# Relative attention: turning one PSUM bank's distances by transposes and the other's by products with the identity

## The reference, cut to what matters

```python
q, k, v = x @ Wq + bq, x @ Wk + bk, x @ Wv + bv        # then split into 8 heads
attn1 = jnp.einsum('bhqd,bhkd->bhqk', rq, rk)
attn2 = jnp.einsum('bhqd,qkd->bhqk', rq, rk2)          # rk2 = rel_k[clipped distance k - q]
attn = jax.nn.softmax((attn1 + attn2) * (1.0 / math.sqrt(c)), axis=-1)
w1 = jnp.einsum('bhqk,bhkd->bhqd', attn, rv)
w2 = jnp.einsum('bhqk,qkd->bhqd', attn, rv2)
out = (w1 + w2).transpose(0, 2, 1, 3).reshape(b, t, c) @ Wo + bo
```

## Time and profile before

| what | value |
|---|---|
| median of 3 timed runs | 2436.7 us (2436.6 to 2438.9) |
| profiled execution, its own time | 2430.69 us |
| its span | 2428.9 us |
| busy share of the span, PE / DVE / ACT / POOL | 90% / 74% / 70% / 24% |
| mean granted clock of TensorE | 0.922 |
| image loop, from its first matmul to DVE's last maximum | 1489.57 to 1615.57 us |

### The profile page before, as it was taken

The page is one execution under the profiler, slowest core; times in us unless marked ns, Lnnn a source line. Parts: engine busy times, 40 slices in busy tenths (PEclk is TensorE's granted clock), DMA queues, the critical chain, the costliest instruction groups (busy, mean ns, idle before and its releaser), DMA issues. The chain is left out here.

```text
span 2428.9 us, 55288 instructions
## 1 busy us (share of the span) xinstructions
PE 2174.1 (90%) x22198; PEld 1519.2 (63%) x22198; DVE 1793.3 (74%) x2576; ACT 1708.1 (70%) x3089; POOL 586.3 (24%) x262
## 2 busy tenths in 40 slices
PE   6689999999999999998746979988599999999998
PEld 3554444444444444443235859865499999999998
DVE  4348999899998998988656344544688888888887
ACT  3478888888888888888742245751677777777776
POOL 0234545454544544444200011430000000000000
PEclk9589999999999999999857977999599999999999
DMA  6287777787787777787510000000321221222220
GB/s 177 74 236 215 217 202 225 214 229 199 219 228 219 214 213 218 218 225 206 121 56 1 2 9 2 2 23 19 121 70 62 73 74 66 73 74 74 74 74 20
DMA packets 113320, 305.66 MB, mean 126 GB/s; under 512 B 20479, under 2 KB 57465, under 8 KB 112554
## 3 DMA queue, kind: packets, MB, share of 16 engines
q1 hardware_dynamic: 113066, 302.13, 43.1%
HBM read 169.11 MB, written 80.65 MB: 103 GB/s over the span
## 5 line engine op out<-in xcount | busy, mean ns | idle before, releaser
L750 ACT ACTIVATE la_hid<-ps,la_b 128x904 f32<-128x904 f32 (+1 forms) x480 | 451.1, 989 | 115.5 <-PE ps L602 114.5
L1721 PE MATMUL ps<-ls_xm,ls_w_in_parts 128*128 128x226 f16 x3072 | 468.3, 262 | 12.1 <-DVE ls_xm L1802 8.6
L1729 PE MATMUL ps<-ls_state_parts,ls_w_rec_parts 128*128 128x226 f16 x2976 | 447.9, 259 | 0.0
L1748 ACT ACTIVATE ls_gates<-ps,ls_bias 128x226 f32<-128x226 f32 x768 | 301.6, 446 | 126.9 <-PE ps L1729 126.8
L602 PE MATMUL ps<-la_pairs,la_w 32*64 32x452 f32 x3584 | 332.9, 592 | 26.4 <-ACT la_hid L750 23.2
L1721 PEld LDWEIGHTS ps<-ls_xm,ls_w_in_parts 128*128 128x128 f16 x3072 | 295.3, 97 | 21.7 <-issue 8.9
L1729 PEld LDWEIGHTS ps<-ls_state_parts,ls_w_rec_parts 128*128 128x128 f16 x2976 | 285.2, 96 | 6.3
L615 PE MATMUL ps<-la_hid,la_w 128*32 128x452 f32 x1856 | 251.8, 579 | 1.0 <-ACT la_opened L756 1.0
L576 POOL TENSOR_TENSOR la_P<-la_S,la_top 113x904 f32<-113x904 f32 x64 | 153.4, 2397 | 266.5 <-DVE la_top L863 266.5
L602 PEld LDWEIGHTS ps<-la_pairs,la_w 32*64 32x64 f32 x3584 | 78.3, 134 | 196.2 <-issue 113.4
L564 POOL TENSOR_TENSOR la_P<-la_P,la_inv 113x904 f32<-113x904 f32 x64 | 153.6, 2420 | 192.7 <-DVE la_inv L842 192.7
(11 more groups left out here) (292 smaller groups left out, 4336.1 us busy)
## 6 DMA issues: line engine op xcount, KB each, us to landing
la_pairs<-la_maps SPq DMA_DIRECT2D x224, 452.0 KB, 6.1
la_gate<-la_opened SPq DMA_DIRECT2D x448, 113.0 KB, 3.5
ls_w_all<-ls_weights SPq DMA_DIRECT2D x32, 904.0 KB, 4.1
la_maps<-la_ST SPq DMA_DIRECT2D x32, 791.0 KB
la_maps<-la_S SPq DMA_DIRECT2D x32, 791.0 KB
ls_m_all<-ls_masks SPq DMA_DIRECT2D x32, 456.0 KB, 3.6
la_maps<-la_Cr SPq DMA_DIRECT2D x32, 395.5 KB
la_maps<-la_Cl SPq DMA_DIRECT2D x32, 395.5 KB
```

The costliest lines, as they stand in the source:

```text
L750: act.activation(hid[:, u % 4, 0:n], ps[:, bank:bank + n, 0:HALF], ACT.Gelu_apprx_tanh, bias=b1[:])\
L1721: mm = pe.matmul(out_j, w_in_parts[:, w, e, j, :], xm[:, t % 2, e, :, x, 0:N], start=((w, x) == PASSES[0]), stop=(t == 0 and (w, x) == PAS ...
L1729: mm = pe.matmul(out_j, w_rec_parts[:, w, e, j, :], state_parts[:, x, e], start=False, stop=((w, x) == PASSES[-1]))
L1748: return act.activation(dst, ps[:, n % 3 * 2 + j // 2, j % 2 * 256:j % 2 * 256 + C], ACT.Tanh if j == 3 else ACT.Sigmoid, bias=bias[:, e, ...
```

## The change

In `distances`, bank 1 is now filled first, by four transposes (`is_transpose=True`), and bank 0 after it, by the same four products with the identity as before. The wait for `raised` stands before bank 1. Everything else is the same: the same blocks, the same PSUM places, the same `start` and `stop`.

```diff
-                def distances(b):
-
-                    if b >= SETS:
+                def distances(b, bank):
+                    if b >= SETS and bank == 1:
                         pe.wait_ge(s["raised"], b - SETS + 1)
-                    for bank in range(2):
-                        for part in range(2):
-                            for t in range(2):
-                                pe.matmul(ps[0:N, 2 * (b % SETS) + bank, slot(part, t)], weights[:, 4 * part + 2 * bank + t, b, :],
-                                          ident[0:N, 0:N], start=(part == 0 and t == 0), stop=False, skip_group_check=True)
+                    for part in range(2):
+                        for t in range(2):
+                            to, x = ps[0:N, 2 * (b % SETS) + bank, slot(part, t)], weights[:, 4 * part + 2 * bank + t, b, :]
+                            if bank == 0:
+                                pe.matmul(to, x, ident[0:N, 0:N], start=(part == 0 and t == 0), stop=False, skip_group_check=True)
+                            else:
+                                pe.matmul(to, x, ident[0:N, 0:N], is_transpose=True, start=(part == 0 and t == 0), stop=False,
+                                          skip_group_check=True)
...
-                        distances(b)
+                        distances(b, 1)
+                        distances(b, 0)
                         scores(b, 0)
```

## The result

The changed kernel takes 2506.98 us (median of 4 runs, 2502.03 to 2512.85) against 2437.34 us (4 runs, 2436.6 to 2438.9): ratio 1.0299, 95% interval 1.0279 to 1.0319, slower by 70 us. The forecast was 2507. Where the runs of a later kernel fell into two groups, the ratio given for it is of the lower group alone.

What follows compares the result with a forecast made beforehand. DVE's maximum, copy, `turn`, `scores` period (3.97 us) bounds the loop, PE at 1.2 GHz after the change. 71.7 + 0.8 = +72.5 us on 2430.7 or 2436.7 gives 2503 or 2509; forecast 2507, range 2433 to 2522.

Steps and rivals of the forecast that it cites:

- Nothing in the loop repeats what raised the clock: Image loop: longest full-width run falls from 3.28 to 2.50 us, so the clock stays at 1.2 GHz; chance 0.60.
- the rise in image 0: Loop's first image before the change: sixteen full-width passes, 3.28 us, raised the clock 0.4 us after their end.
- The price at 1.2 GHz: Image loop at the low clock: 4.70 us an image without `turn`, 6.33 with it, 197.7 us instead of 126.0.
- The sum: Whole kernel at the low clock: 71.7 + 0.8 = +72.5 us.
- the slower `turn` at the end: Tail of the image loop: one `turn` goes from 1.02 to 1.83 us at 1.2 GHz, adding 0.8 us.
- The part at 2.4 GHz: Image loop at full clock: four fewer passes an image, hidden behind DVE's copy from image 4 on; -1.8 us.
- The full 13 us: Image loop at 2.4 GHz: 32 x 0.41 us of PE work saved if DVE's copy did not cover it.
- the circle: Image loop: DVE's maximum, reciprocal, copy, PE's `turn`, second `scores`, next maximum; sets 3.97 us an image.
- The clock rises anyway: Rival, image loop: clock rises within some three images, so 2435 us, no change; chance 0.17.
- Transposes don't hold the clock: Rival, image loop: the clock falls again even after a rise, ending near 2500 us; chance 0.05.
- sixteen transposes ahead of the rise at 110.9: Earlier in the kernel: a transpose run at 106.67, then other full-width work; cited as evidence that transposes count.
- The gap rival: PE's gap ahead of `far_scores`: the clock does not fall there before the loop, 2421 us; chance 0.07.

Runs made afterwards that it cites:

- Raised from outside: Changed kernel with 16 more full-width products (results not used) on PE right ahead of the image loop: 2433.19 us, ratio 1.0004.
- sixteen passes of mixed kind: Changed kernel with the four transposes of bank 1 made twice over, eight of sixteen passes being transposes: 2434.04 us, ratio 1.0003.
- twelve of pure products: Kernel before, with the products of part 1 in bank 1 left out and no transposes: 2512.85 us, ratio 1.0327.
- both gaps filled: Changed kernel with two full-width products in PE's wait before `far_scores` and two more ahead of its last chunk: 2414.05 us, ratio 0.9912.
- `turn` was out of the circle: Changed kernel, both gaps filled, `turn(b - 3)` moved behind `scores(b, 1)`: 2400.79 us; the same with products in both banks: 2413.51 us.

## Why the prediction was right

- **The clock, the step on which it all hung.** "Nothing in the loop repeats what raised the clock": shown from three sides. Raised from outside, the changed loop keeps the clock; sixteen passes of mixed kind raise it; twelve of pure products don't. The prediction took the rise in image 0 from a single profile. With products in the first three images a run of sixteen failed to raise it once in the profile and, by their times and mean clocks, three times in a row in four executions of ten. So what each image lost with four of its sixteen passes is a chance of the rise, not a certain one.
- **The price at 1.2 GHz.** An image without `turn` was put at 4.70 us and measures 4.76 (1495.99 - 1491.23, the starts of L1355 of two images early in the changed loop), one with `turn` at 6.33 and measures 6.41. The loop, to the last maximum, takes 200.4 us (forecast 197.7) against 126.0. The 0.08 an image that is missing is the sum of three errors, by the starts in the timeline of one image: `distances` takes 2.55 us (put at 2.50), `turn` 1.79 (put at 1.63), the two `scores` together 2.07 (put at 2.20). For `turn` the likely reason is that the row it was taken from had no change to narrow passes behind it; here each of the four changes of form shows 0.20 us of idle weight load.
- **The sum.** The spans differ by 2500.3 - 2428.9 = 71.4 us, forecast 72.5: 74.4 in the loop, 0.1 behind it, and 3.1 less before it, since this execution's loop began at 1486.50 instead of 1489.57, which is no work of the change. So the loop was put 2.7 us too low, and a start that happened to be early gave it back: that the median came out at the very number is luck, the size of the loss is not. The 0.8 us for the slower `turn` at the end did not come: from the last maximum to `far_values` it is 11.6 us against 11.4, as ACT's exponentials cover most of it.
- **The part at 2.4 GHz.** -1.8 us, no difference: with the clock raised ahead of the loop the ratio is 1.0004, and the saved time stands as a wait before `turn`. Between loops at full clock, the changed one with both gaps filled against the kernel before with one, it is 124.3 - 122.7 = 1.6 us. The full 13 us came out once `turn` was out of the circle.
- **The rivals.** "The clock rises anyway" did not happen in any of the four runs. "Transposes don't hold the clock" is refuted for this loop: PEclk was 1.00 over 121.8 us with twelve transposes an image. The Trainium skill (TensorE: Matmul & The Clock Gate, Part 4: PE-mode transpose) says that a transpose does not count as busy in the way a matmul does; this loop's trace disagrees. The prediction's own ground, sixteen transposes ahead of the rise at 110.9, was thin, since other full-width work stood between them and the rise. The loop without any full-width product leaves open whether transposes and narrow products alone would hold the clock for long. The gap rival named the right place: filling the gap is worth 13 us in the kernel before by the ratio, 16 between the profiled executions. It lacked one thing that I had not seen, the second gap.

## What to carry to other kernels

Before removing PE work, ask at which clock the stage is entered and which run of passes raised it: a saving of 10% in passes cost 60% of the stage here, because the removed passes were the ones that brought the clock up. An engine that is busy 99% of a loop need not be its bound; follow one period around, and compare an iteration in which a wait is missing. A short idle gap of PE ahead of a long stretch of narrow matmuls is worth filling with full-width work of no use, and in the changed kernel filling the first gap alone gave back 13 us of the 70; only with the second filled too did the loop keep the clock.

## What I had not expected of the hardware

The clock has a memory in both directions. The same narrow matmuls of `far_scores` ran 39.1 us at 1.2 GHz without rising and, after a filled gap, 25 us at 2.4 GHz without falling. Hence one program can have two times 70 us apart in this loop (2426 to 2439 us and 2503 to 2507 us with products for the first three images). What decides between them in an execution is not shown; the moment at which the runs of passes fall is my guess. Single waits of PE of 1.48 or 1.49 us stood shortly ahead of a fall of the clock in three kernels, but the same 1.48 us with a run of sixteen passes behind it did not bring it down, and neither did waits of 0.42 us in nearly every image over 122 us.
